# Cross-attention with a routed FFN on one core: the second normalisation's transposition, logits and positions of a group come three steps later, with four record buffers in place of three

## The reference, cut to what matters

```python
x = x + tanh(g_xattn) * attention(layernorm(x), ctx, ctx)   # 16 heads of width 8
x = x + tanh(g_ffn) * moe(layernorm(x))                     # 8 experts, capacity 512

# moe, for the 4096 tokens as one list:
logits = tokens @ Wg                       # [4096, 8]
gates = softmax(logits); idx = argmax(gates, axis=1)
mask1 = one_hot(idx)
locations1 = cumsum(mask1, axis=0) - 1.0   # place of a token in its expert's list
# token -> row locations1 of expert idx, if under the capacity
hidden = relu(expert_in @ W1 + b1); expert_out = hidden @ W2 + b2
out = gate * expert_out, back at the token's own place
```

## Time and profile before

| | before |
|---|---|
| runs, us | 354.29, 354.58, 359.06 |
| profiled execution, us | 352.81 |
| its span, us | 351.0 |
| TensorE busy | 261.1 us (74%) |
| VectorE busy | 201.8 us (57%) |
| ScalarE busy | 158.5 us (45%) |
| GpSimd busy | 173.4 us (49%) |
| chain that ended last | GpSimd 26%, issue 26%, TensorE 22%, ScalarE 8%, VectorE 7%, DMA 5% |

### The profile page before, as it was taken

One profiled execution on the slowest core, in us unless ns is written; L12 is line 12 of the kernel. 1 busy time (PEld: TensorE's weight loads), 2 busy tenths in 40 slices (PEclk: granted clock), 3 DMA queues, 4 the chain that ended last, 5 costly groups with the idle time before them and its releaser, 6 DMA issues.

```text
span 351.0 us, 8166 instructions
## 1 busy us (share of the span) xinstructions
PE 261.1 (74%) x2960; PEld 169.0 (48%) x2960; DVE 201.8 (57%) x696; ACT 158.5 (45%) x357; POOL 173.4 (49%) x202
## 2 busy tenths in 40 slices
PE   0348698888996995996896888969331899999920
PEld 0124445545654654654654555635220366777720
DVE  6244649778895895568687597932320144544520
ACT  7253376865764763564674456551010332322100
POOL 5336724757179179238728625070462005555572
PEclk9999999999998998589899699995555699999985
DMA  2984765615244235208217111074014225664300
GB/s 79 294 222 110 229 183 149 182 32 162 64 115 129 66 91 152 63 3 230 51 29 209 43 56 64 5 200 76 30 51 130 71 64 162 186 200 142 89 37 21
DMA packets 48536, 39.26 MB, mean 112 GB/s; under 512 B 9619, under 2 KB 44072, under 8 KB 48497
## 3 DMA queue, kind: packets, MB, share of 16 engines
q1 hardware_dynamic: 44784, 28.67, 30.5%
q0 software_dynamic: 3712, 10.07, 8.6%
HBM read 13.72 MB, written 12.65 MB: 75 GB/s over the span
## 4 chain that ended last, share of the span: by engine, by line
POOL 26%; issue 26%; PE 22%; ACT 8%; DVE 7%; DMA 5%; SPq 2%; POOLq 1%; ACTq 0%; DVEq 0%
POOL rec_dram L1002 7%; POOL out_dram L1056 6%; POOL rs L982 4%; PE O L489 3%; PE X L418 3%; ACT prob L623 2%; ACT xn L615 2%; DVE negm L734 2%; POOL rec L988 2%; PE S L460 2%; POOL rec L990 2%; PE X L412 2%; PE TS L561 2%; PE X L435 2%; DMA qp<-parts_q 2%
## 5 line engine op out<-in xcount | busy, mean ns | idle before, releaser
L734 DVE TENSOR_REDUCE negm<-S 128x4 f32<-128x512 f32 x128 | 81.8, 680 | 27.5 <-PE S L460 26.5
L623 ACT ACTIVATE prob<-TS 128x512 f32<-128x512 f32 x128 | 72.0, 589 | 47.5 <-PE TS L475 47.3
L489 PE MATMUL O<-prob,vals 128*32 128x128 f32 x1024 | 58.1, 303 | 1.6 <-ACT oraw L632 1.6
L460 PE MATMUL S<-kp,qp 62*128 62x128 bf16 x512 | 33.5, 234 | 5.2 <-DVE negm L734 4.7
L1056 POOL DMA_INDIRECT out_dram<-fin,tok x32 | 31.3, 979 | 11.2 <-issue 11.2
L1002 POOL DMA_INDIRECT rec_dram<-rec,slot x32 | 31.8, 994 | 9.7 <-issue 9.7
L256 POOL TENSOR_TENSOR rest_k<-full_k,parts_k 128x512 f32<-128x512 f32 x7 | 8.1, 1155 | 53.4 <-ACT parts_k L606 53.4
L489 PEld LDWEIGHTS O<-prob,vals 128*32 128x32 f32 x1024 | 21.3, 113 | 21.7 <-issue 10.9
L975 POOL TENSOR_TENSOR fence_p<-pool_c 128x1 f32<-128x1 f32 x16 | 3.1, 194 | 56.7 <-DVE fin L955 34.3
L460 PEld LDWEIGHTS S<-kp,qp 62*128 62x128 bf16 x512 | 19.2, 100 | 23.5 <-issue 11.7
L475 PE MATMUL TS<-qp,kp 64*128 64x128 bf16 x512 | 28.9, 228 | 1.3 <-DMA qp<-mrow 1.3
(11 more groups left out here) (115 smaller groups left out, 513.1 us busy)
## 6 DMA issues: line engine op xcount, KB each, us to landing
kp<-parts_k SPq DMA_DIRECT2D x48, 128.0 KB
qp<-parts_q SPq DMA_DIRECT2D x48, 128.0 KB, 2.7
rec_dram<-zeros POOLq DMA_DIRECT2D x8, 516.0 KB
xr<-rec_dram SPq DMA_DIRECT2D x8, 260.0 KB, 2.9
c_sb<-in_ctx_dram SPq DMA_DIRECT2D x8, 256.0 KB, 4.4
out_dram<-rec SPq DMA_DIRECT2D x8, 256.0 KB
w1s<-in_L_ffn_W_dram SPq DMA_DIRECT2D x8, 256.0 KB, 3.1
w2s<-in_L_ffn_W_dram SPq DMA_DIRECT2D x8, 256.0 KB, 2.9
```

The lines of the kernel that those rows point to most:

```text
L460: mm = nc.tensor.matmul(S[:, a, i * L:(i + 1) * L], qp[b][rows, h, t0:t0 + L], kp[b][rows, h, t0:t0 + L], start=True, stop=True)
L489: mm = nc.tensor.matmul(o_out[i * HV:(i + 1) * HV, u * L:(u + 1) * L], vals[G % 2][:, k, h, :], prob[n % 2][:, h * L:(h + 1) * L], start=( ...
L623: nc.scalar.activation(prob[n % 2][:, first:first + 4 * L], TS[:, a, :], ACT.Exp).then_inc(a_exp, 1)
L734: V.tensor_reduce(negm[n % 2][:, first:first + 4], S[:, a, :].rearrange("p (h k) -> p h k", k=L), AX.X, ALU.max, negate=True).then_inc(v_r ...
```

## The change

The transposition `nT` of group G moves from step 4G+9 to 4G+12, the logits with `route` from 4G+10 to 4G+13, and the positions with `place` from 4G+11 to 4G+14. The scatter of group G moves from 4G+11 to 4G+15, or later in GpSimd's order by one group's work; the special place for the scatter of group 6 goes, and the order of GpSimd's last instructions (norm2 of group 7, scatter of 6, scatter of 7) stays. There are four buffers of records and slots, and the zeroing transfers are counted on four semaphores. The second normalisation itself stays where it was. `moments2` has one more wait, for GpSimd's norm2 of the group before. The steps end at 43, not 39.

```diff
-    FIRST, LAST = -8, 4 * (NG - 1) + 11
+    FIRST, LAST = -8, 4 * (NG + 2) + 3
+    RB = 4
...
-        rec = [sb(f"rec{i}", [P, GB, REC]) for i in range(3)]
+        rec = [sb(f"rec{i}", [P, GB, REC]) for i in range(RB)]
...
-            third = {2: ("lg", g - 2), 3: ("pos", g - 2)}.get(j)
+            third = {1: ("lg", g - 3), 2: ("pos", g - 3)}.get(j)
...
-            second = {1: ("nT", g - 2), 2: ("xT", g + 2), 3: ("q", g + 2)}.get(j)
+            second = {0: ("nT", g - 3), 2: ("xT", g + 2), 3: ("q", g + 2)}.get(j)
...
-                if j == 1 and is_group(g - 2):
-                    G = g - 2
+                if j == 0 and is_group(g - 3):
+                    G = g - 3
                     act.wait_ge(p_nT, G + 1)
                     nc.scalar.activation(xn2T[:], X[:, 0, :], ACT.Copy).then_inc(a_nT, 1)
...
-                if n % GB == 0 and G >= 3:
-                    dve.wait_ge(sent[G % 3], zeros_sent(G % 3) + 16 * GB * (G // 3))
-                    dve.wait_ge(x1_out[G % 3], 16 * (G // 3))
+                if n % GB == 0 and G >= RB:
+                    dve.wait_ge(sent[G % RB], zeros_sent(G % RB) + 16 * GB * (G // RB))
+                    dve.wait_ge(x1_out[G % RB], 16 * (G // RB))
...
             def moments2(G):
                 dve.wait_ge(v_st2, GB * G + GB)
+                if G >= 1:
+                    dve.wait_ge(g_xn2, G)
...
-                if j == 2 and is_group(g - 2):
-                    logits(g - 2)
-                if j == 3 and is_group(g - 2):
-                    positions(g - 2)
-                if j == 2 and is_group(g - 2):
-                    route(g - 2)
-                if j == 3 and is_group(g - 2):
-                    place(g - 2)
+                if j == 1 and is_group(g - 3):
+                    logits(g - 3)
+                    route(g - 3)
+                if j == 2 and is_group(g - 3):
+                    positions(g - 3)
+                    place(g - 3)
...
-                if j == 0 and g - 3 == NG - 2:
-                    scatter(NG - 2)
...
-                if j == 3 and is_group(g - 2) and g - 2 != NG - 2:
-                    scatter(g - 2)
+                if j == 3 and is_group(g - 3):
+                    scatter(g - 3)
```

More of the change, by code:

```diff
@@ L148, in flamingo_kernel @@
         base = sb("base", [P, GB])
-        slot = [sb(f"slot{i}", [P, GB], U32) for i in range(3)]
+        slot = [sb(f"slot{i}", [P, GB], U32) for i in range(RB)]
         w1s = [sb(f"w1s{i}", [P, F]) for i in range(2)]
@@ L172, in flamingo_kernel @@
         q_in, k_in = [sem(f"q_in{i}") for i in range(3)], [sem(f"k_in{i}") for i in range(3)]
-        x1_out = [sem(f"x1_out{i}") for i in range(3)]
-        sent = [sem(f"sent{i}") for i in range(3)]
+        x1_out = [sem(f"x1_out{i}") for i in range(RB)]
+        sent = [sem(f"sent{i}") for i in range(RB)]
         p_cT, p_xT, p_q, p_k, p_v = sem("p_cT"), sem("p_xT"), sem("p_q"), sem("p_k"), sem("p_v")
@@ L264, in zeros_sent @@
         def zeros_sent(p):
-            return 16 * len(range(p, ZEROED, 3))
+            return 16 * len(range(p, ZEROED, RB))
         def run_steps(step_fn):
@@ L371, in load_xr @@
                 sp.dma_start(xr[e % 2][:], rec_v[e][:, :, D:REC]).then_inc(xr_in[e % 2], 16)
-            for p in range(3):
-                sp.wait_ge(sent[p], zeros_sent(p) + 16 * GB * len(range(p, NG, 3)))
+            for p in range(RB):
+                sp.wait_ge(sent[p], zeros_sent(p) + 16 * GB * len(range(p, NG, RB)))
             for e in range(2):
@@ L391, in _ @@
                 load_xr(e)
-            for p in range(3):
-                sp.wait_ge(x1_out[p], 16 * len(range(p, NG, 3)))
+            for p in range(RB):
+                sp.wait_ge(x1_out[p], 16 * len(range(p, NG, RB)))
             for p in range(2):
@@ L862, in place @@
                 V.scalar_tensor_tensor(base[:], choice[:], float(CAP), loc[:], ALU.mult, ALU.add).then_inc(v_place, 1)
[L864 removed]
+                V.reciprocal(rec[G % RB][:, :, 2 * D], lsum[:])
                 done(2)
[L866 removed]
+                V.tensor_tensor(slot[G % RB][:], base[:], over[:], ALU.add).then_inc(v_slot, 1)
             def step(c):
@@ L992, in scatter @@
             def scatter(G):
-                p = G % 3
+                p = G % RB
                 if G == 0:
-                    for q in range(3):
+                    for q in range(RB):
                         pool.wait_ge(sent[q], zeros_sent(q))
@@ L1057, in rows_out @@
                                           bounds_check=T - 1, oob_is_err=False).then_inc(fin_out[p], 16)
-            for p in range(3):
-                pool.wait_ge(x1_out[p], 16 * len(range(p, NG, 3)))
+            for p in range(RB):
+                pool.wait_ge(x1_out[p], 16 * len(range(p, NG, RB)))
             for e in range(E):
```

20 lines of the change are left out of this document (9 added, 11 removed).

## The result

The changed kernel took **365.4 us** (median of 4 runs, 363.12 to 367.4) against 356.65 us of the kernel before beside it (4 runs): ratio **1.032 [1.027, 1.037]**, slower, where 349.7 us and a range of 344 to 356 were forecast. Some executions of a kernel run longer at a lower granted clock: the times of kernels given here are medians of all their timed runs, and the ratios are taken from the faster runs alone, so a ratio can differ a little from the quotient of the medians. The profiled execution took 363.12 us, its span is 361.3 us; before they were 352.81 and 351.0. In the changed kernel most lines are one to three higher: L798 is now L801, L990 is L991, L606 is L607, L430 is L431.

The account below looks back on a forecast made before the run. It took waits for GpSimd, chiefly TensorE's 23.0 us for its normalisation, as the bound. Terms summed to -4.9 us from the profiled 352.81, so 347.9; with 1.77 for the median of runs, 349.7 us, range 344 to 356.

Parts of the forecast that it names:

- step 25's routing: Step 25: VectorE's routing, ahead of the next maxima, is held up beside GpSimd until 197.35; +0.8 us.
- steps 26 to 31: Steps 26 to 31: older group's logits and place computation leave, -1.0; step 29's wait goes and its step shortens, -1.0 us.
- steps 33 to 36: End of the attention: the 3.45 us wait goes, transposition and logits lie earlier and cost less; -4.8 us.
- They fit, just. I take +0.2 each: Steps 17 and 21: routing needs 0.9 us and fits the 1.2 us of four-element GpSimd instructions; +0.2 us each.
- the routing too late for the gap: Rival, 0.09: maxima of steps 17 and 21 end past 136.6, routing meets the query split; +3.8 each, 357.3 us.
- 0.4 each, -1.2 in all: Steps 14-15, 18-19, 22-23: logits leave, positions move to the middle step; only work after the `xn` transposition shortens.
- The clock's rival: Rival, 0.22: TensorE's clock stays up from step 17, as it then stands under 2 us for `oraw`; -4.4, 345.3 us.
- Step 13, +0.7: Step 13: routing between maxima and offset loses up to four 512-element GpSimd lengths, so the offset ends later; +0.7 us.
- The end, +1.2: Behind the last projection: group 6's and 7's routing run there, the last two scatters follow back to back; +1.2 us.
- The root blocks too: Rival, 0.13: GpSimd's root instruction also holds up the routing in steps 17 and 21; +2.3 twice, 354.3 us.
- the rule as the prediction tells it: A VectorE instruction with two SBUF inputs contends with any GpSimd instruction that reads SBUF.
- Blocking is rare: Rival, 0.09: GpSimd gives way between instructions; steps 13 and 25 bring back waits of 3.8 and 4.2 us; 341.7 us.

Follow-up runs that it names:

- record: The first measurement of the changed kernel beside the kernel before: 365.4 us against 356.65 us, ratio 1.032.
- e17: The kernel before, unchanged, one execution on chip D for its profile: 350.09 us.
- e18: The changed kernel, unchanged, measured again on chip D: 348.6 us, ratio 0.990 to the kernel before.
- e3: The changed kernel with routing operands (logits, ordinals, count) read from PSUM, chip A: 349.3 us, ratio 0.986 to the kernel before.
- e12: The code of e3 again, on chip B: 337.9 us, ratio 0.962 to the kernel before.
- e7: The kernel before with only its routing operands read from PSUM, chip A: 360.0 us, ratio 1.012.
- e5: e3 with GpSimd's scatter moved behind its second normalisation, in step 4g+4, chip A: 357.3 us, ratio 0.994 to the kernel before.
- e6: e3 without its record scatters (one record to a fixed row for each), chip A: 326.6 us, ratio 0.917 to the kernel before.
- e8: The kernel before without its record scatters (one record to a fixed row for each), chip A: 326.2 us, ratio 0.917.
- e10: e3 with a group's four indirect transfers spread over four steps, chip B: 328.3 us, ratio 0.936 to the kernel before.
- e13: The kernel before with only the four indirect transfers spread over four steps, chip C: 333.5 us, ratio 0.947.
- e14: The changed kernel, routing from SBUF, with the four indirect transfers spread over four steps, chip C: 347.9 us, ratio 0.979 to the kernel before.
- e16: The code of e10 again, on chip C: 328.9 us, ratio 0.940 to the kernel before.
- e4: The changed kernel with transposition, logits with routing, and positions all one step later, chip A: 360.3 us, no ratio (executions 349.5 to 366.7).

## Why the prediction was wrong, point by point

The starts of the same instructions, counted from the first residual, us:

| | before | changed, record | before, D (e17) | changed, D (e18) |
|---|---|---|---|---|
| residual 20 (step 25) | 129.8 | 137.4 | 126.8 | 131.7 |
| residual 28 (step 33) | 173.0 | 186.0 | 170.2 | 172.7 |
| residual 31 (last) | 189.9 | 195.8 | 187.2 | 182.6 |
| last scatter | 206.0 | 214.5 | 203.3 | 200.8 |
| end of the span | 291.6 | 302.0 | 289.0 | 285.8 |

The first residual itself stood at 59.3 to 59.4 us, in e18 at 62.0. Taken apart by stretch, changed less before:

| from, to | forecast | record | chip D |
|---|---|---|---|
| first residual to residual 20 (steps 13 to 23) | -0.1 | +7.6 | +4.9 |
| to residual 28 (step 25's routing, steps 26 to 31) | -1.2 | +5.4 | -2.4 |
| to residual 31 (steps 33 to 36) | -4.8 | -7.2 | -7.0 |
| to the last scatter | +1.2 | +2.6 | +2.1 |
| to the end (the experts) | 0 | +2.0 | -0.7 |

**The step that failed: "They fit, just. I take +0.2 each" (steps 17 and 21).** From the keys' first part to the offset's end were 15.3 us; after, 18.25 (125.03 to 143.28) and 18.2 (155.37 to 173.55), +3 each. My own rival named it, the routing too late for the gap, with 0.09: the maxima should end past 136.6, and they ended at 139.5, which is 137.9 on the old scale, since the keys stand 1.6 us later here. But it had no cause for them to be late by that much, and TensorE's late results were it. They came in three more places in the second half (ScalarE's waits of 2.22, 4.12 and 3.91 us in steps 25 to 32) and in three in the experts' stage (VectorE's 11.1 us before `yb`), for which I had no term at all. On chip D, without them, the same stretch is 15.4 us (127.57 to 142.97) against 15.3: there the +0.2 was right. The forecast's only profile has no late results, so nothing that it read could show them.

**The second step that failed: "0.4 each, -1.2 in all" (steps 14 and 15, 18 and 19, 22 and 23).** From the offset's end to the next keys' first part the kernel before took 11.3, 15.7 and 11.3 us, the changed kernel 14.2, 12.1 and 12.1; on chip D 11.6 to 11.9 became 14.1, 13.1 and 14.2. In the record that is +0.2 in sum, since the kernel before has its own slow stretch in the second place; on chip D the -0.4 became +1.2 to +2.5 each, +6.0 in sum, which is all of the first stretch's +4.9 and more. In the record that stretch is the two late routings (+5.8) and the late results of step 25 (+2.9).

**The premise.** I read that two waits end within 1.1 us of each other in steps 13, 17 and 21, and credited nothing for the first; that was right, and the second took its place in full: TensorE stood 4.09 us for `oraw` (e18), where I had said "under 2 us". What I did not do was ask what makes GpSimd's row long. The scatter is 4.9 us of it (127.96 to 132.86); spread, it is worth five times what the change gave on chip D.

**The clock's rival went the other way.** I gave 0.22 to a clock that stays up. After, half clock was granted for longer in steps 13 to 25 than in the earlier trace rows (a mean of 0.80 against 0.88), and on chip D too (0.84 against 0.87); e3 had 0.91 and e12, without late results, 0.96. Windows of 6 us behind the offset, busy time by engine and granted clock, e18 and then e3:

```profile
145.00:151.00 6.00, 5.80 (x76) 3.76 (x75) 3.54 (x16) 3.93 (x9) 1.52 (x2) 0.50 0.34 92
```

```profile
137.00:143.00 6.00, 5.89 (x91) 3.62 (x90) 4.59 (x19) 5.51 (x15) 2.38 (x2) 0.88 0.24 61
```

At 1.2 GHz TensorE is as busy with 76 matmuls as at nearly 2.4 GHz with 91. In the stretch of the second failed step e3 needs 10.9, 10.9 and 11.5 us. So "-0.4 each" holds in the first two passes of e3 (granted clock 1.00 and 0.88 over the stretch; in e18 it was 0.64, 0.74 and 0.64), and where the clock was at half for longer it became a loss. What brings the half clock on was not tested by itself: in e18 the 4.09 us of standing still come just before; e12 stood 3.07 us there (until 138.03), was granted 0.72 from 136.6 to 142.6 and 1.00 in the 6 us after.

**Step 13, +0.7.** Three of the five two-input instructions were held up, not four lengths in a row: one that begins in the gap between two GpSimd instructions passes (L832, 0.18 us). From keys to the offset's end, -0.4 (14.96 against 15.36).

**Steps 33 to 36, -4.8.** More came: from residual 28 to 31 16.97 us before, 9.82 after (-7.2), and 16.99 against 9.97 on chip D. It is the largest gain of the change, a little beyond the end of -6.8 that I had kept for it.

**The end, +1.2.** From the last residual to the last scatter: +2.6, on chip D +2.1, inside the ends of 0 and +3.5. The two scatters are not back to back, since group 7's slots are begun 0.1 us after group 6's last instruction ends (268.97 and 268.88), and its own first transfer starts 1 us behind them.

**The other rivals.** The root blocks too: no, L837 took 0.21 us inside L983 (e18), as the fence did inside L982 in the earlier trace rows, although these GpSimd instructions read SBUF too; so the rule as the prediction tells it is too wide for the root's four elements. Blocking is rare: no, the changed kernel was held up in each of steps 13, 17, 21 and 25. (Two of the rivals' times are a little off in their sums: without blocking 341.0 and not 341.7, with the late routing 356.9 and not 357.3; no chance or bound hangs on it.)

In sum the change gave -3.2 us on chip D, counted from the first residual, against the -4.9 of the forecast; that the two are near is luck, since the terms are others. In the record's profiles it gave +10.4, and most of the 13 us between the two lie in the late results and in the routing that they push into the split. Part of this may not be the change's: the record's profile before has no late results even in the experts' stage, whose code the change leaves alone, while its profile after has 11.1 us of them there. So the two were probably not taken under the same condition, and whether the kernel before has late results on the record's chip is not shown; e7 says that on chip A the same order, with its routing from PSUM, has them. The medians give an estimate: the kernel before took 354.6 and 357.8 us on chip A and 350.8 to 351.6 on B, C and D, the changed one 365.4 in the record and 348.6 on C and D. If the record's chip was like A, late results cost the order before 3 to 7 us and the changed order 17.

## What to carry to other kernels

When a wait is found, follow the engine waited for to all who stand behind it, and ask what makes its row long: a wait that ends 1 us before another is worth nothing alone, and spreading the four indirect transfers (0.947 for the kernel before, with nothing else changed) did what reordering their neighbours could not (0.99 to 1.03). Two-input VectorE instructions beside GpSimd's elementwise work are cured by an operand in PSUM more surely than by finding them a gap, since a gap of 1.2 us does not outlive a delay of 3 us upstream. And a change of one per cent is to be measured on more than one chip: this one was 3.2 per cent slower in one place and 1.0 per cent faster on another chip, and neither interval holds 1.

## What the runs showed of the hardware

- **TensorE's results come late beside indirect transfers issued in a row, on some chips.** In the record's profile and in all six of chip A with such scatters in the steps, scores given to TensorE reached ScalarE after waits of 1.9 to 5.5 us, where it is 0.4 us at that place in e18 and 0.8 in the kernel before; in the five of chips B, C and D with four transfers in a row there is no such wait in the whole trace. They move with the scatter (e5) and go from the steps without it (e6, e8); in the experts' stage, where the output is scattered in rows of four, all eight profiles of chip A have one to three such waits of VectorE, e6 and e8 too (4.4 and 4.0 us), and none of chips B, C and D has. With one transfer per step (e10, e13, e14, e16) there are none, but that was run on chips B and C alone, which never had any, so it is open whether the spread cures them. The cause is open: in the windows of the late results in the changed kernel, e3 and e4 the granted clock was full (1.00) and the DMA engines as busy (0.78 to 0.95) as in the kernel before (0.75 to 0.99). The Trainium skill, "SBUF — State Buffer", section "Who interferes with whom", says that PE and ACT never wait on anyone; it says so of the ports of SBUF, and these rows show a delay that it does not cover.
- **The mean granted clock of a whole execution says little of its time:** e6 and e8 ran at 0.886 and 0.941, both in 326 us. They differ in their order too, so this is no price of the clock.
- **What is held up depends on what GpSimd runs when the instruction begins:** of the five two-input VectorE instructions in each of the steps 13, 17, 21 and 25 of the changed kernel, L829 and L837 stood until a 512-element GpSimd instruction ended (1.19 and 0.89 us), and so did L828 (1.01 us in the first two, 0.37 and 0.34 in the others); L832 and L833, which began between two of them, took 0.18 and 0.15. Beside the four-element L983 the same L837 took 0.21 us (e18).
